# A decoder layer on one core: biased exponentials per head for the decay, DVE's linked operations as single steps, another split of the gelu sessions, new queue orders

## The chip, the cores and the metric

One core of one Trainium2 chip runs the whole program once. The metric is device time in microseconds (us) of that core; lower is better. Engines are named as in the profile: PE (TensorE), DVE (VectorE), ACT (ScalarE), POOL (GpSimd), and SP, which only issues DMAs.

## The reference

Input x is 16 samples of 128 tokens by 128 features, and there is a context of the same shape. One decoder layer with three layernorms is computed:

```
x = LN(x + attn(x))                 # 16 heads of 8; Q and K through a k=3 convolution and a projection
                                    # scores*tau + delta, with tau, delta = sigmoid(conv(gelu(dwconv(x))))
x = LN(x + xattn(x, ctx, ctx))      # mLSTM: 4 heads of 32
                                    #   D = exp(logD - max), C = qk*D/sqrt(32)
                                    #   norm = max(|sum C|, exp(-max logD)); per-head layernorm
x = LN(x + ffn(x))                  # blocks of 32 quantised to FP6 (scale = max|x|/7.5), one 128x128 linear
```

## The kernel before

Attention goes sample by sample (16), everything behind it group by group. `GR` lists 9 groups: seven of two samples (0 to 6), two of one (7 and 8). Projections and the convolution branches go by chunks of four samples (0 to 3). Every engine runs its own list of steps written out by hand (`PE_ORDER`, `DVE_ORDER`, `ACT_ORDER`, `POOL_ORDER`, `SP_ORDER`); a step is `name.index`. An engine takes its list strictly in order and each step waits on semaphores, so a step that is not ready holds up everything behind it on that engine.

**Front.** `tx.c` transposes chunk c of x on PE. `tapT`/`tapD` (two per chunk and branch, 16 in all) are the depthwise convolution: POOL writes the first tap, line 343, and DVE adds the two others, lines 995 and 996. `geT`/`geD` are the gelus on ACT (line 466), `tau`/`del` the projections on PE (lines 704, 713), `thT`/`thD` the tanh on ACT, `edx` exp(delta), `edT`/`edc` its transposition and copy. `K`, `Q` are projections of 6 matmuls each (line 627); `kf`, `qf` add the bias on DVE; `qs` multiplies q by tau; `km`, `qm` are masked copies for four heads on POOL (line 296). Gelu and exp lie in different activation tables: `gelu` and `exp` load one. The first table session is gelu for chunks 0 to 2, `exp.0` follows, then later `gelu.1`, the steps of chunk 3, and `exp.1`. POOL's tap for a chunk c from 2 on waits for `tau`/`del` of chunk c-2, whose buffer it takes. `zeros.0` (lines 333 to 335) clears the value buffers on POOL.

**Attention loop.** For sample n, `aa`/`v1`/`v2` hold the scores of n (`score_a`, line 633) and those of n-2 less their maximum (`score_b`, line 639, `less_max`, line 645) in four PSUM banks. `mX`/`mY` on DVE take the maxima (line 1054), `split` on POOL splits them into three bf16 parts, `nmT` transposes them, `eX`/`eY` on ACT are the exponentials (line 507), and `pv` (line 847, 64 small matmuls) multiplies by the values `vz` (DVE) and `ez` (POOL). `rec`, `att`, `y1` finish a group's attention (line 857 and 858).

**Behind it, for each group.** `y1s`, `sq1` (first layernorm), `yT`, `gb`, `l1`, `lf`, `gF`, `scan` (gates, cumulated); `spread` on SP writes the gate row to DRAM and reads it back on all partitions; `dm` on POOL masks it (line 391) and adds the column term g (line 393, 1024 columns); `dec` on ACT is one exponential of 1024 columns (line 560). Groups 7 and 8 (`BY_ROWS`) get their decay from PE (`ld`) and four exponentials with g as bias (line 567). `qk`, `cc` (decay times scores, DVE), `hst` (line 911), `hs`, `hq`; then `nrm`, `vs`, `rh`, `z2`, `bn`, `qa`, `zb` on DVE (with `rh`, `std` on ACT), `xd` (POOL), `dT`, `ffn` (PE), `z3` (DVE), `sq3` (ACT), `yo` (POOL, line 426) and `store` (SP). `cT`, `cm`, `gc` bring in the context. `warm.k` is k matmuls whose result nobody reads (line 917), all behind the last `att`.

`link(ins)` makes DVE wait for the instruction just issued; with it the steps `nrm` (3 links), `vs`, `z2`, `gb`, `bn`, `qa` (4) hold chains of small dependent operations within one step.

## Time and profile before

| | us |
|---|---|
| median of 3 runs | 234.24 |
| lowest and highest | 232.49, 236.56 |
| the profiled execution, its own time | 234.09 |
| its span, first to last instruction | 232.3 |
| PE busy | 206.4 (89%) |
| DVE busy | 169.7 (73%) |
| ACT busy | 128.6 (55%) |
| POOL busy | 115.2 (50%) |
| mean granted clock of PE | 0.977 |

A busy share is an average over the span; the front, the attention loop and the end have different limits. PE's digits in the profile's 40 slices run 2889397799799989998999999999997989999991, DVE's 2699999997824433559846798598697459998981.

### The profile page before, as it was taken

The page shows a single profiled execution, that of the slowest core. Times are in us where ns is not written, and L with a number is a line of the kernel's source. Part 1 is how long each engine was busy: PE and PEld are TensorE (multiplying, and loading weights), DVE is VectorE, ACT ScalarE, POOL GpSimd, SP SyncE. Part 2 cuts the span into 40 slices and gives each one's busy share as a digit, 9 for nine tenths or more (in the row PEclk, how much of TensorE's full clock was granted, in tenths as well). Part 3 has the DMA queues.
Part 4 walks back from the last instruction along what each step waited for, and adds up shares of the span by engine and source line. Part 5 has one row for each costly group of instructions (what it writes and reads, how often), then busy time and mean ns, then how long its engine had stood idle before and what let it go on. Part 6 is the DMA issues. An engine that isn't in the chain of part 4 may idle for free.

```text
span 232.3 us, 6553 instructions
## 1 busy us (share of the span) xinstructions
PE 206.4 (89%) x2377; PEld 137.6 (59%) x2377; DVE 169.7 (73%) x429; ACT 128.6 (55%) x365; POOL 115.2 (50%) x225
## 2 busy tenths in 40 slices
PE   2889397799799989998999999999997989999991
...
DVE  2699999997824433559846798598697459998981
...
GB/s 172 179 122 1 3 0 1 0 4 0 0 48 0 4 93 0 3 94 1 48 5 26 1 91 93 25 4 0 116 5 3 90 115 7 0 1 25 23 30 18
DMA packets 11311, 8.43 MB, mean 36 GB/s; under 512 B 2736, under 2 KB 10384, under 8 KB 11280
## 3 DMA queue, kind: packets, MB, share of 16 engines
...
HBM read 6.94 MB, written 1.08 MB: 35 GB/s over the span
## 4 chain that ended last, share of the span: by engine, by line
DVE 35%; PE 35%; issue 17%; POOL 7%; ACT 5%; POOLq 0%; DVEq 0%; ACTq 0%
PE bankPV L847 9%; PE score L633 6%; DVE u L995 5%; DVE u L996 4%; DVE nm L1054 4%; PE bankY L911 2%; PE score L639 2%; DVE z L1185 2%; PE bankP L704 2%; PE bankP L774 2%; PE score L645 2%; POOL qm L296 2%; DVE z L1164 1%; DVE mT L1157 1%; DVE hn L1140 1%
## 5 line engine op out<-in xcount | busy, mean ns | idle before, releaser
L1054 DVE TENSOR_REDUCE nm<-score 128x8 f32<-128x1024 f32 x32 | 38.8, 1219 | 9.3 <-PE score L633 9.3
L507 ACT ACTIVATE prob<-score 128x1024 f32<-128x1024 f32 x32 | 32.5, 1019 | 22.9 <-PE score L645 22.7
L633 PE MATMUL score<-km,qf 32*128 32x512 f32 x128 | 34.1, 642 | 1.2 <-DVE nm L1054 1.2
L639 PE MATMUL score<-qm,kf 32*128 32x512 f32 x128 | 34.3, 645 | 0.1
L466 ACT ACTIVATE u<-u,db 128x512 f32<-128x512 f32 x16 | 11.3, 719 | 19.0 <-DVE u L996 19.0
L645 PEld LDWEIGHTS score<-nmT,sel 32*128 32x128 bf16 x256 | 10.3, 95 | 16.7 <-issue 16.5
L296 POOL TENSOR_SCALAR km<-kf,mcol 128x512 f32<-128x512 f32 x16 | 13.9, 888 | 10.8 <-DVE kf L1031 5.6
L847 PE MATMUL bankPV<-prob,vz 128*32 128x128 f32 x512 | 18.7, 289 | 0.0
L917 PE MATMUL bankPV<-maskb,identb 128*128 128x512 bf16 x73 | 17.8, 380 | 0.0
L847 PE MATMUL bankPV<-prob,ez 128*32 128x128 f32 x512 | 17.3, 275 | 0.0
L627 PE MATMUL bankP<-xTp,wT 128*128 128x512 f32 x36 | 16.8, 602 | 0.4 <-ACT dth L476 0.4
L372 POOL CAST nmx<-nm 128x16 bf16<-128x16 f32 x16 | 3.2, 201 | 27.5 <-issue 19.7
L995 DVE SCALAR_TENSOR_TENSOR u<-xTp,dw,u 128x512 f32<-128x512 f32 x16 | 14.8, 927 | 2.2 <-POOL u L343 2.2
L911 PEld LDWEIGHTS bankY<-ctm,xt 128*128 128x128 f32 x128 | 15.1, 192 | 1.3 <-issue 0.8
L399 POOL TENSOR_SCALAR x<-y1s,rs 128x128 f32<-128x128 f32 x16 | 5.8, 375 | 20.1 <-DVE z L1164 14.0
L911 PE MATMUL bankY<-ctm,xt 128*128 128x33 f32 x128 | 15.8, 277 | 0.0
L343 POOL TENSOR_SCALAR u<-xTp,dw 128x512 f32<-128x512 f32 x16 | 13.9, 879 | 3.8 <-ACT xTp L454 2.7
L426 POOL TENSOR_SCALAR abT<-z,rs 128x128 f32<-128x128 f32 x16 | 5.9, 378 | 19.2 <-ACT rs L613 19.2
L847 PEld LDWEIGHTS bankPV<-prob,vz 128*32 128x32 f32 x512 | 14.1, 115 | 2.1 <-issue 0.8
L996 DVE SCALAR_TENSOR_TENSOR u<-xTp,dw,u 128x512 f32<-128x512 f32 x16 | 14.4, 902 | 0.6
L847 PEld LDWEIGHTS bankPV<-prob,ez 128*32 128x32 f32 x512 | 14.7, 112 | 0.1
L296 POOL TENSOR_SCALAR qm<-qf,mcol 128x512 f32<-128x512 f32 x16 | 12.6, 804 | 4.2 <-DVE qf L1041 4.2
...
## 6 DMA issues: line engine op xcount, KB each, us to landing
...
```

The costliest lines, as they stand in the source:

```text
L296: ins = nc.gpsimd.tensor_scalar(dst[:, CB * (c % 2):CB * (c % 2 + 1), j, :], src[:, CB * c:CB * (c + 1), :], mcol[:, j:j + 1], 1.0, ALU.mu ...
L507: nc.scalar.activation(prob[:, i % 2, k:k + 2, :].rearrange("p k s -> p (k s)"), sc[:, 512 * k:512 * (k + 2)], ACT.Exp, scale=SQ_SCALE).th ...
L627: ins = mm(place(name), wT[:, n, k, :], xTp[:, CB * c:CB * (c + 1), k:k + S], start=(k == 0), stop=(k == TAPS - 1))
L633: ins = mm(sc[:, 512 * k:512 * (k + 1)], qf[r, n, :], km[r, n % (2 * CB)].rearrange("p j s -> p (j s)"), start=True, stop=True)
L639: mm(sc[:, 512 * k:512 * (k + 1)], kf[r, n, :], qm[r, n % (2 * CB)].rearrange("p j s -> p (j s)"), start=True, stop=False)
L645: ins = mm(sc[:, 512 * k + S * j:512 * k + S * (j + 1)], sel[r, j, :], nmT[r, n % 3, :], start=False, stop=(j == J - 1))
L847: ins = mm(pvb[32 * k:32 * (k + 1), o:o + S], w[:, G * (i % 4) + k, 32 * j:32 * (j + 1)], prob[:, i % 2, k, S * j:S * (j + 1)], start=(j = ...
L911: ins = mm(yb[:, o:o + CW], cc[:, i % 2, S * k:S * (k + 1)], ctm[:, b0 + v, h, :], start=True, stop=True)
L917: mm(pvb[:], identb[:], maskb[:].unsqueeze(1).to_broadcast([P, NH, S]), start=True, stop=True)
L995: link(nc.vector.scalar_tensor_tensor(o, xTp[:, cs, 0:S], dw[:, n, j, 0:1], o, ALU.mult, ALU.add))
L996: nc.vector.scalar_tensor_tensor(o, xTp[:, cs, 2:S + 2], dw[:, n, j, 2:3], o, ALU.mult, ALU.add).then_inc(taps_done[n], 1)
L1054: nc.vector.tensor_reduce(nm[:, i % 3, J * k:J * (k + 2)], sc[:, 512 * k:512 * (k + 2)].rearrange("p (h s) -> p h s", s=S), AX_X, ALU.max, ...
```

## The change

1. `dm` keeps only its mask on POOL. `dec` for groups 0 to 6 becomes 8 exponentials of 128 columns, each with one column of g as bias, in place of one of 1024 columns. The groups 7 and 8 stay as they were.
2. The steps of DVE that held links are cut up: `gb` into `gb ga`; `nrm` into `na nb nrm`; `vs` into `v0 vs`; `z2` into `za z2`; `bn` into `ba bn be`; `qa` into `q0 q1 q2 q3 qa`. Each part has a semaphore, waits for the part before, and can stand anywhere in DVE's list. `hn8` and `st` get two buffers, so that waits for the group before become waits for the one before that. One of the four operations of `nrm` (maximum with the negated sum) goes; ACT takes the absolute value in a new step `ha` (128x8).
3. Gelu sessions: the first holds chunk 0 (`geT.0 geT.1 geD.0 geD.1`, and `geD.2`), then `exp.0` and four score exponentials of samples 0 and 1, then `gelu.1` with all other gelus and tanhs, then `exp.1`.
4. All five lists are new. `warm` falls from 73 matmuls to 46.

```
 PE_ORDER (before, first lines)
-    tx.0 ab.0 hw.0 mT.0 mT.1 wT.0 tx.1 del.0 tx.2 wT.1 tau.0 K.0 del.1 Q.0 Q.1 tx.3 del.2 aa.0 Q.2 gw.0 aa.1 tau.1 cg.0 nmT.0 ow.0 v1.2 nmT.1 K.1 edT.0
-    v2.2 edT.1 K.2 v1.3 V.0 edT.2 rc.0 v2.3 nmT.2 cT.0 pv.0 cm.0 v1.4 cm.1 pv.1 nmT.3 v2.4 V.1 y1.0 v1.5 nmT.4 tau.2 v2.5 gF.0 pv.2 v1.6 nmT.5 pv.3 tau.3
-    yT.0 del.3 MT.0 K.3 v2.6 edT.3 ...
+    tx.0 ab.0 mT.0 mT.1 hw.0 tx.1 tx.2 tx.3 wT.0 cT.0 wT.1 del.0 K.0 Q.0 tau.0 Q.1 gw.0 edT.0 aa.0 aa.1 K.1 nmT.0 cg.0 v1.2 nmT.1 ow.0 Q.2 v2.2 rc.0 K.2
+    v1.3 nmT.2 v2.3 K.3 del.1 nmT.3 tau.1 del.2 v1.4 tau.2 V.0 tau.3 pv.0 del.3 pv.1 V.1 v2.4 edT.1 cm.0 y1.0 edT.2 v1.5 edT.3 V.2 pv.2 yT.0 v2.5 nmT.4
...
 PE_ORDER (last lines)
-    v1.15 nmT.14 pv.12 v2.15 y1.5 cm.7 pv.13 nmT.15 bb.14 dT.3 cm.8 y1.6 gF.5 qk.4 ffn.3 MT.5 pv.14 yT.5 bb.15 gF.6 hst.4 qk.5 MT.6 y1.7 yT.6 pv.15 hst.5
-    yT.7 qk.6 y1.8 warm.6 gF.7 warm.8 dT.4 ld.7 ffn.4 warm.3 gF.8 qk.7 hst.6 warm.4 dT.5 ld.8 ffn.5 MT.7
-    warm.8 hst.7 warm.3 yT.8 warm.5 MT.8 qk.8 warm.5 dT.6 warm.4 ffn.6 warm.5 hst.8 warm.4 dT.7 warm.4 ffn.7 warm.14 dT.8 ffn.8
+    cm.7 v1.15 nmT.14 hst.3 dT.2 v2.15 ffn.2 cm.8 gF.5 qk.4 pv.13 MT.5 bb.14 nmT.15 hst.4 qk.5 y1.6 dT.3 pv.14 yT.6 bb.15 ffn.3 gF.6 y1.7 qk.6 pv.15 MT.6
+    hst.5 dT.4 y1.8 yT.7 warm.1 ffn.4 yT.8 warm.3 gF.7 warm.4 ld.7 qk.7 MT.7 hst.6 gF.8 qk.8 hst.7 dT.5 ld.8 MT.8 ffn.5 warm.5 hst.8 warm.8 dT.6 warm.3
+    ffn.6 warm.7 dT.7 warm.2 ffn.7 warm.11 dT.8 warm.2 ffn.8

 DVE_ORDER (first lines, and from the last att on)
-    cent.0 sel.0 ab.0 tapT.0 tapD.0 hw.0 mT.0 tapD.1 mT.1 tapT.1 wT.0 bias.0 tapD.2 tapT.2 tapD.3 tapT.3 wT.1 tapT.4 bias.1 kf.0 tapD.4 qf.0 tapD.5 qs.0
-    qf.1 tapT.5 wd.0 mY.0 mX.0 qf.2 gw.0 mX.1 mY.1 cg.0 qs.1 tapD.6 mX.2 tapD.7 ow.0 kf.1 tapT.6 mY.2 tapT.7 kf.2 mX.3 vz.0 rc.0 mY.3 gc.0 mX.4 ...
-    z2.4 gb.7 bn.4 att.8 qa.4 lf.7 nrm.5 zb.4 vs.5 scan.7 cc.6 gb.8 z2.5 lf.8 bn.5 z3.4 qa.5 scan.8 zb.5 cc.7 nrm.6 vs.6 z2.6 z3.5 bn.6 dd.7 qa.6 nrm.7
-    dd.8 vs.7 zb.6 cc.8 z2.7 bn.7 z3.6 qa.7 zb.7 nrm.8 vs.8 z3.7 z2.8 bn.8 qa.8 zb.8 z3.8
+    cent.0 sel.0 ab.0 tapT.0 mT.0 mT.1 tapD.0 hw.0 tapD.1 wT.0 tapD.2 wT.1 tapT.1 bias.0 wd.0 bias.1 kf.0 qf.0 tapT.2 tapD.3 qs.0 tapD.4 mX.0 mY.0 qf.1
+    gw.0 mY.1 mX.1 tapD.5 cg.0 kf.1 mX.2 ow.0 tapT.3 qf.2 tapT.4 mY.2 rc.0 tapT.5 mX.3 kf.2 mY.3 kf.3 qs.1 tapT.6 tapD.6 mX.4 tapT.7 tapD.7 vz.0 qs.2 ...
+    q3.4 qa.4 zb.4 gb.7 dd.6 att.8 ga.7 lf.7 v0.5 na.5 nb.5 nrm.5 vs.5 z3.4 gb.8 ga.8 za.5 z2.5 ba.5 scan.7 bn.5 cc.6 q0.5 lf.8 be.5 q1.5 dd.7 q2.5 q3.5
+    qa.5 cc.7 zb.5 scan.8 na.6 v0.6 nb.6 nrm.6 vs.6 v0.7 za.6 na.7 z2.6 nb.7 dd.8 ba.6 z3.5 cc.8 bn.6 nrm.7 q0.6 vs.7 be.6 q1.6 q2.6 q3.6 za.7 qa.6 z2.7
+    zb.6 na.8 ba.7 nb.8 v0.8 nrm.8 bn.7 vs.8 q0.7 be.7 q1.7 q2.7 z3.6 za.8 q3.7 qa.7 zb.7 z2.8 ba.8 z3.7 bn.8 q0.8 be.8 q1.8 q2.8 q3.8 qa.8 zb.8 z3.8

 ACT_ORDER (first lines)
-    xT.0 geT.0 geD.0 geD.1 xT.1 thD.0 geT.1 xT.2 geD.2 thT.0 geT.2 geD.3 geT.3 thD.1 geT.4 geD.4 geD.5 xT.3 thD.2 geT.5 thT.1 nmT.0 exp.0 edx.0 edx.1 ...
+    xT.0 geT.0 xT.1 xT.2 geD.0 xT.3 geD.1 cT.0 geD.2 thD.0 geT.1 thT.0 exp.0 edx.0 edc.0 nmT.0 eY.0 nmT.1 eX.0 eY.1 nmT.2 eX.1 gelu.1 geD.3 geT.2 geD.4
+    geT.3 thD.1 geT.4 nmT.3 geT.5 geD.5 thT.1 thD.2 geT.6 geD.6 thT.2 geT.7 geD.7 thT.3 thD.3 exp.1 eY.2 edx.1 rec.0 edx.2 edx.3 eX.2 edc.1 cm.0 y1s.0
...
 POOL_ORDER (first lines)
-    ident.0 consts.0 tapT.0 tapD.0 tapT.1 tapD.1 zeros.0 tapD.2 tapT.2 tapD.3 tapT.3 tapT.4 tapD.4 tapT.5 tapD.5 km.0 qm.0 split.0 tapD.6 split.1 tapD.7 ...
+    ident.0 consts.0 tapT.0 zeros.0 tapD.0 tapT.1 tapD.1 tapT.2 tapD.2 tapT.3 tapD.3 km.0 tapD.4 tapT.4 qm.0 tapT.5 split.0 tapD.5 ez.0 ez.1 split.1 km.1
+    split.2 xr.0 xr.1 xr.2 xr.3 km.2 split.3 tapT.6 tapD.6 tapT.7 qm.1 tapD.7 split.4 ez.2 x1.0 qm.2 split.5 ez.3 x1.1 split.6 km.3 dm.0 split.7 ez.4
```

```
 POOL, dm
-                    pool.wait_ge(g_done, i + 1)
                     t = dec[:, i % 2, 0:w * S].rearrange("p (h s) -> p h s", s=S)
-                    link(nc.gpsimd.affine_select(... fill=MASKED ...))
-                    nc.gpsimd.tensor_tensor(t, t, g[:, i % 2, 0:w].unsqueeze(2).to_broadcast([P, w, S]), ALU.add).then_inc(dm_done, 1)
+                    nc.gpsimd.affine_select(... fill=MASKED ...).then_inc(dm_done, 1)
 ACT, dec
-                    nc.scalar.activation(t, t, ACT.Exp).then_inc(dec_done, 1)
+                    for k in range(NH * GR[i][1]):
+                        t = dec[:, i % 2, S * k:S * (k + 1)]
+                        ins = nc.scalar.activation(t, pb[:, S * k:S * (k + 1)] if i in BY_ROWS else t, ACT.Exp, bias=g[:, i % 2, k:k + 1])
 ACT, new step ha
+                    nc.scalar.activation(ha[:, i % 2, 0:w], hs[:, i % 2, 0:w, DH], ACT.Abs).then_inc(ha_done, 1)
 DVE, nrm (before: four operations with three links)
-                    link(nc.vector.scalar_tensor_tensor(h1, hv, -1.0, h0, ALU.mult, ALU.max))
 DVE, qa (before: subtraction, link, quantise with three links inside); now
+                elif name == "q1":
+                    dve.wait_ge(q0_done, i + 1)
+                    nc.vector.tensor_reduce(qs8[:, i % 2, 0, 0:4 * nb], z[...], AX_X, ALU.max, apply_absolute_value=True).then_inc(q1_done, 1)
...
```

## Rows read from the trace of the kernel before

**Rows 1.** Busy time by stretch: window, its length, then each engine (instructions).
```profile
0.00:73.40 73.40, 58.49 (x442) 35.31 (x442) 57.51 (x107) 26.07 (x46) 51.38 (x93) 0.95 0.16 42
73.40:195.70 122.30, 116.59 (x1728) 82.62 (x1728) 83.09 (x218) 82.91 (x237) 53.45 (x113) 0.99 0.12 39
195.70:232.30 36.60, 31.30 (x210) 19.71 (x209) 29.10 (x106) 19.65 (x83) 10.35 (x21) 0.99 0.05 15
```

**Rows 2.** What PE waited for between 73.4 and 198.3 us: total, times, longest.
```profile
PE bankT L865 <- DVE dd L1122: 1.1, 1, 1.1
```

**Rows 3.** Timeline of PE: start, duration, work; first score of sample 5.
```profile
73.41 0.70 PE L633 MATMUL score<-km,qf 32*128 32x512 f32 x2
```

**Rows 4.** Timeline of PE: two context projections, then tau.3, del.3 and K.3.
```profile
65.88 0.73 PE L774 MATMUL bankP<-cen,cT 128*128 128x136 f32 x4
...
83.95 1.98 PE L704 MATMUL bankP<-u,xd 128*128 128x512 f32 x4
...
86.81 0.64 PE L713 MATMUL bankP<-u,d2w 128*32 128x128 f32 x16 [0.65 <-ACT th L472]
...
88.02 2.81 PE L627 MATMUL bankP<-xTp,wT 128*128 128x512 f32 x6 [0.42 <-ACT dth L476]
```

**Rows 5.** Groups of DVE instructions by line: count, busy us, mean ns, idle before.
```profile
L1054 DVE TENSOR_REDUCE nm<-score 128x8 f32<-128x1024 f32 x32 | 38.8, 1219 | 9.3 <-PE score L633 9.3
L995 DVE SCALAR_TENSOR_TENSOR u<-xTp,dw,u 128x512 f32<-128x512 f32 x16 | 14.8, 927 | 2.2 <-POOL u L343 2.2
L996 DVE SCALAR_TENSOR_TENSOR u<-xTp,dw,u 128x512 f32<-128x512 f32 x16 | 14.4, 902 | 0.6
```

**Rows 6.** Timeline of DVE: the first vz.
```profile
60.32 0.47 DVE L1068 TENSOR_TENSOR vz<-bankP,ed 128x128 f32<-128x128 f32 x2
```

**Rows 7.** POOL: the last memset of zeros.0 (timeline).
```profile
13.44 2.24 POOL L335 MEMSET ez<- 128x2560 f32 x1
```

**Rows 8.** POOL: groups by line, masks and the decay.
```profile
L296 POOL TENSOR_SCALAR km<-kf,mcol 128x512 f32<-128x512 f32 x16 | 13.9, 888 | 10.8 <-DVE kf L1031 5.6 <-PE score L633 5.1
L393 POOL TENSOR_TENSOR dec<-dec,g 128x1024 f32<-128x1024 f32 x7 | 13.6, 1940 | 0.6
```

**Rows 9.** Timeline of PE: del.1, then the six matmuls of Q.0.
```profile
27.05 1.08 PE L713 MATMUL bankP<-u,d2w 128*32 128x128 f32 x16 [3.45 <-issue]
28.17 3.89 PE L627 MATMUL score<-xTp,wT 128*128 128x512 f32 x6
```

**Rows 10.** Groups of ACT instructions by line: decay, exponentials, table loads.
```profile
L507 ACT ACTIVATE prob<-score 128x1024 f32<-128x1024 f32 x32 | 32.5, 1019 | 22.9 <-PE score L645 22.7
L560 ACT ACTIVATE dec<-dec 128x1024 f32<-128x1024 f32 x7 | 7.4, 1051 | 3.3 <-POOL dec L393 3.3
L459 ACT ACT_TABLE_LOAD x2 | 2.6, 1283 | 0.0
L567 ACT ACTIVATE dec<-bankP,g 128x128 f32<-128x128 f32 x8 | 2.3, 363 | 0.0
L480 ACT ACTIVATE dth<-dth,halfc 128x128 f32<-128x128 f32 x4 | 1.4, 391 | 0.0
```

**Rows 11.** Timeline of ACT: four per-head exponentials of group 7.
```profile
204.39 1.13 ACT L567 ACTIVATE dec<-bankP,g 128x128 f32<-128x128 f32 x4
```

**Rows 12.** Timeline of POOL: the decay's addition in group 4.
```profile
170.08 2.16 POOL L393 TENSOR_TENSOR dec<-dec,g 128x1024 f32<-128x1024 f32 x1
```

**Rows 13.** Timeline of DVE in the same stretch.
```profile
170.52 2.00 DVE L1164 TENSOR_TENSOR z<-mT,x 128x256 f32<-128x256 f32 x1
```

**Rows 14.** Timeline of DVE from the last att on.
```profile
195.70 0.29 DVE L1076 TENSOR_TENSOR att<-bankPV,rec 128x128 f32<-128x128 f32 x1
195.91 2.09 DVE L1185 TENSOR_SCALAR z<-z,mv 128x128 f32<-128x128 f32 x2
...
210.17 0.17 DVE L1141 SCALAR_TENSOR_TENSOR hn<-hn,se 128x8 f32<-128x8 f32 x1
...
226.55 0.29 DVE L949 TENSOR_TENSOR x<-z,qs 128x128 fp8e4<-128x128 f32 x1
```

More of the change, by code:

```diff
@@ L80 @@
-    thT.2 nmT.5 geD.7 thT.3 yT.0 thD.3 exp.1 eY.4 edx.3 em.0 rec.1 dec.0 eX.4 edc.3 y1s.1 sq1.1 eY.5 nmT.6 l1.1 eX.5 hs.0 hq.0 eY.6 em.1 rh.0 rec.2 nmT.7
-    eX.6 std.0 cT.1 dec.1 yT.1 eY.7 cT.2 dT.0 eX.7 nmT.8 cm.2 sq3.0 rec.3 nmT.9 cm.3 eY.8 cm.4 y1s.2 sq1.2 yT.2 y1s.3 l1.2 sq1.3 eX.8 l1.3 hs.1 hq.1 cm.5
-    rh.1 nmT.10 eY.9 std.1 eX.9 dec.2 em.2 rec.4 dT.1 cT.3 eY.10 em.3 cm.6 sq3.1 nmT.11 eX.10 dec.3 hs.2 yT.3 hq.2 eY.11 nmT.12 rh.2 eX.11 std.2 y1s.4
-    sq1.4 nmT.13 eY.12 l1.4 rec.5 dT.2 sq3.2 eX.12 em.4 hs.3 hq.3 yT.4 eY.13 nmT.14 rh.3 eX.13 std.3 dec.4 y1s.5 cm.7 sq1.5 nmT.15 rec.6 l1.5 eX.14 dT.3
```

197 lines of the change are left out of this document (118 added, 79 removed).

## The prediction

> **What bounds the kernel now.** Read the busy time by stretch first [rows 1]. I cut the span at the first score of sample 5 (`v1.5`, 73.41 us [rows 3]) and at the last `att` (195.70 [rows 14]). In the middle PE is busy for 116.6 of 122.3 us, DVE for 83.1, ACT for 82.9: PE bounds it, and of PE's 5.7 us of rest only a few are waits with a name, the longest 1.1 us for a `dd` that stood behind linked operations on DVE [rows 2]. In the front DVE is busy for 57.5 of 73.4 us, 29.2 of them the 16 pairs of taps [rows 5]; it is short of 100% only because the first eight and the last ten us are poor in DVE work. In the end, 36.6 us, DVE is busy for 29.1 with 106 small instructions, and ACT for 19.7. So three sums are needed: how early PE is filled, what is left of waits in the middle, how long DVE's list is behind the last `att`.
>
> **Front: new order and gelu sessions.** I take differences against the old list. Before the first `vz` (60.32 [rows 6]) old DVE had done 16 tap pairs, seven maxima, `kf`/`qf` 0 to 2, `qs` 0 and 1. New DVE up to `mY.3` has 12 pairs, eight maxima, no `qs.1`, and also `rc.0`. With the rows' means: minus 4 x 1.83 (927 and 902 ns), plus 1.2, minus 0.9, plus about 1.0 for `rc.0` (an estimate for its small operations), minus 2.2 that DVE waited for POOL's first taps [rows 5]. New is a wait for `tapD.0`: `zeros.0` is ahead of it on POOL, whose two memsets are 2.24 us each [rows 7], and of these 4.5 us DVE covers three with `tapT.0`, `mT.0`, `mT.1`; plus 1.6. `mY.3` then ends near 53.7.
>
> Here the new order has a chain. On POOL `km.2` (4 x 0.67 undisturbed, 0.89 on average [rows 8]) and `split.3` (about 1) follow; PE has `nmT.3` before `tau.1`; from the start of a `tau` to the end of its tanh it is 2.9 us (83.95 to 86.81 [rows 4]); `qs.1` waits for that, and so do POOL's `tapT.6`, which takes `tau.1`'s buffer, and the three other taps of chunk 3. That is 53.7 + 3.3 + 1 + 0.2 + 2.9 + 0.9 = 62.0 after `qs.1`, with DVE idle for some 6 us. Four tap pairs, `mX.4` and half a `vz`: + 7.3 + 1.2 + 0.3 = 70.8. ACT may leave the gelu session only after `thD.3`: `pv.0` about 2, `del.3` with its tanh 1.2 (86.81 to 88.02 [rows 4]), table 1.28, `eY.2` 1.02, three `edx` of 0.39 and one `rec` 0.8, `eX.2` 1.0 [rows 10]: `v1.5` starts at 79.3, minus 0.7 because `nmT.3` and `km.2` overlap DVE's `kf.3`: **78.6**, 5.2 later than now.
>
> But PE has more behind it by then: `tau.2` and `tau.3` (1.83 each, 83.95 to 85.78 where the next begins), `del.3` 0.6, `K.3` 2.8, and the waits of 0.65 and 0.42 beside them [rows 4], together 8.1, less `cm.1`, 0.7. That is 7.4 us that the middle no longer holds. **Front: 5.2 - 7.4 = -2.2 us.** Bounds: a pass over 512 columns cannot well take less than half of the 1.22 us of a maximum over 1024 [rows 5]; 15 pairs at 1.22 instead of 1.83 are 9.2 us less, so -11; on the other side, if each pair's two passes were held as long again as POOL's mask, 0.89 [rows 8], in 7 of the 15, 6.2 us later, so +4. I take the rows' mean, because POOL's masks and first taps still run beside these taps.
>
> **Middle: linked steps, POOL's addition, per-head exponentials.** POOL loses 7 x 1.94 = 13.6 us [rows 8]. It is not bound by these, but DVE was held up by them: `z2` of group 4, which begins 0.44 us after POOL's addition, took 2.00 us [rows 12, 13]. Nothing but the mask is left there. In a chain the links give one operation each 0.20 us, from 210.17 to the next [rows 14]; now other steps can stand between them. All this pays only where PE waits for DVE: the top wait was 1.1 [rows 2], all that PE was not busy is 5.7 [rows 1], of which 1.07 are counted above. So at most 4.6 are to be had.
>
> Against it stands ACT. One `dec` of 1024 columns is 1.05 us [rows 10]; four per-head ones of 128 columns are 1.13 together [rows 11], one every 0.26, so eight are 2.2: +1.1 for each of 7 groups, 7.7 in all. `ha`, nine of about 0.2: 1.8. ACT goes from 128.6 to about 138 busy. In the middle it is 83 of 122 and would be 90: not a bound in itself, but nothing else runs during a `dec`, and `eX.7`, `nmT.7` and `eX.11` are right behind one. The cover is that exponentials waited 22.9 us for PE in all [rows 10], not PE for them. If that cover were gone, five `dec` in the stretch would cost 5.5 us. The single instruction is 0.36 us from PSUM, and 0.39 for the nearest one from SBUF [rows 10]; both were issued overlapping. DVE's `ga`, `na` and so on have the same number of waits as the links had: no cost. **Middle: -1 us, between -4.6 and +5.5**: I take a quarter of the waits as gone, since the other engines have hardly less to do than before.
>
> By the Trainium skill, *ScalarE: Activation LUTs*, section "What ACT_TABLE_LOAD costs", an exponential with a per-partition bias has a fixed cost of 280 ns and 0.833 ns per column, and neighbours overlap by 93 ns. From that, eight are an estimated 2.44 us, and the seven decays would cost ACT 9.7 us instead of 7.7. The sum would stay, since ACT's time is covered; only the rival below would begin earlier.
>
> **End.** From the last `att` to the end of the last `qa` DVE now takes 195.70 to 226.84, 31.1 us, nearly always at work [rows 1, 14]. Taken out of this piece: `qa.4`, whose subtraction lasted 2.09 beside POOL's addition and which ends 3.4 us after it begins, `zb.4` 0.5, `gb.7` 0.2, and four times one linked operation, 0.8 [rows 14]: 4.9. Interleaving the rest (v0.7, na.7 between the steps of group 6, and so on) hides perhaps one in five of 40 links of 0.1: 0.8. Chain: `cc.8` and `hst.8` are now in front of `dT.6` and `ffn.6` on PE, so the last group is not late. From `qa.8` to the end stays 5.5 (226.84 to 232.30 [rows 1, 14]). **End: -5.5 us**, between 0 (what DVE no longer does is replaced by waits for `l1.8` and `dec.8`, two of which ACT serves later) and -9.
>
> **Sum.** -2.2 - 1 - 5.5 = -8.7: span 232.3 to 223.6. The profiled execution was 234.09, 1.8 over its span; it is 0.15 under the median. So 225.4; I say **225.5**.
>
> **Rivals.**
> - *The front pays as the lists intend.* DVE's taps are little disturbed and the wait for `tau.1` is short. For: taps and `km` no longer coincide everywhere. Against: the chain `km.2`, `split.3`, `nmT.3`, `tau.1`, `qs.1` is in the lists. Front -7, half way to its bound, end -7: 225.4 - 6.3 = 219.
> - *Nothing is gained.* PE gets its work earlier, but starves between 70 and 79 us, and the end stays bound by the chain of `ffn`, `sq3`, `yo`. Front 0, middle +2, end -3: 233. Part of it may be PE's clock: after 3.45 us without a matmul the six of `Q.0` took 3.89 us, those of `K.3` 2.81 [rows 9, 4], the lower of two levels (1.2 against 2.4 GHz) for part of it. In the end 27 of 73 `warm` are gone; if such a gap opens before `hst.7`, `hst.8` or `dT`, each costs about 1 us, four cost 4: 229.5. The Trainium skill says the same of idle stretches (*TensorE: Matmul & The Clock Gate*, "What's actually happening": idle, the array falls to 1.2 GHz); the granted clock now is 0.99 in the end [rows 1].
> - *ACT becomes the bound, slower than before.* Its place is each `dec` ahead of an `eX`, `eY` or `nmT` for which PE is ready. Price: eight at 0.39 not overlapping are 3.1, 2.1 more than one of 1.05 [rows 10]; seven and `ha` are 14.6 + 1.8 = 16.4 us: 225.4 + 16.4 = 242. It decides (over 239) once 13.5 of these are on the path. For: ACT is in order and PSUM banks of scores are freed by it alone. Against: one every 0.26 [rows 11], and ACT idle for 39 of 122 us [rows 1].
> - That the edit doesn't do what it says is not to be expected: it is instruction by instruction.
>
> **How the numbers follow.** Forecast, 221 to 229.6: 0.51. Front pays, 215 to 221: 0.16. Nothing gained, 229.6 to 238.9: 0.25. ACT the bound, above: 0.08. A change within 2% (229.6 to 238.9) could hardly be told from none. Faster 0.67, same 0.25, slower 0.08. The range 217.5 to 234 leaves out some 5 in 100 below, and 15 above: the last rival and the worse end of the one before. The forecast's own range is 221 to 229.6.
>
> **What would show it.** Right: `v1.5` between 76 and 80 us with `tau.3` and `K.3` before it, and a DVE gap of several us before `qs.1`; the last `att` near 193; from there to the end 31 us; no DVE operation of 2 us in the middle; eight exponentials in 2.2 us. Wrong: `v1.5` before 74 (front larger), named waits of PE for ACT of over 3 us in the middle (the third rival), or an end of over 34 us with DVE idle for more than 6 of them.

## The result and the profile after

The changed kernel takes 237.84 us (median of 4 runs, 236.12 to 240.90), the one before 234.07 beside it: a ratio of 1.019, with an interval of 1.013 to 1.025. The prediction was 225.5, range 217.5 to 234. It is slower, by an amount near the 2% that I took as the limit, and it lies outside the range. The profiled execution took 237.81 us, its span is 235.9 (before 232.3). In some executions of a kernel PE's mean granted clock is lower and the time some per cent longer: medians below are over all runs, ratios leave such runs out.

The span cut at the same two events as in [rows 1], the first score of block 5 (`v1.5`) and the last `att` (window, length, busy us of PE, its weight loads, DVE, ACT and POOL, each with its instructions, then granted clock, DMA share and GB/s):

```profile
0.00:88.83 88.83, 70.69 (x469) 41.88 (x469) 56.98 (x108) 32.44 (x54) 49.43 (x92) 0.94 0.13 35
88.83:199.39 110.56, 107.38 (x1717) 79.00 (x1716) 78.67 (x219) 84.12 (x278) 42.37 (x108) 0.98 0.12 38
199.39:235.90 36.51, 29.99 (x169) 19.55 (x168) 22.71 (x94) 20.73 (x93) 8.99 (x19) 0.84 0.11 33
```

`v1.5` comes 15.4 us later than before. 7.4 of these are work taken over from the middle, as in the prediction; 8.0 are a loss. The middle is 11.7 us shorter, 7.4 of it that work, so it gains 4.3. The end has 6.4 us less to do on DVE and is as long as before, with a granted clock of 0.84 in place of 0.99.

The front of the changed kernel in the timeline (start, duration, engine, line, work, and in brackets the idle time before and what ended it), from the table load on that opens the second gelu session:

```profile
59.42 1.28 ACT L458 ACT_TABLE_LOAD   x1
...
65.83 2.90 POOL L346 TENSOR_SCALAR u<-xTp,dw 128x512 f32<-128x512 f32 x3 [3.93 <-PE bankP L710]
66.38 0.69 DVE L1047 SCALAR_TENSOR_TENSOR qf<-th,qf 128x512 f32<-128x512 f32 x1 [4.54 <-ACT th L473]
...
71.56 0.72 ACT L467 ACTIVATE u<-u,db 128x512 f32<-128x512 f32 x1 [1.47 <-DVE u L1002]
...
73.00 0.68 PE L790 MATMUL bankP<-wvT,xTp 128*128 128x128 f32 x4 [2.38 <-ACT th L473]
...
75.72 0.48 DVE L1074 TENSOR_TENSOR vz<-bankP,ed 128x128 f32<-128x128 f32 x2
...
76.34 3.75 PE L710 MATMUL bankP<-u,xd 128*128 128x512 f32 x4 [2.66 <-DVE vz L1074]
80.02 1.40 PE L853 MATMUL bankPV<-prob,vz 128*32 128x128 f32 x32
...
83.20 1.28 ACT L460 ACT_TABLE_LOAD   x1
...
84.49 1.02 ACT L508 ACTIVATE prob<-score 128x1024 f32<-128x1024 f32 x1
...
85.66 0.70 PE L639 MATMUL score<-km,qf 32*128 32x512 f32 x2 [0.54 <-ACT prob L508]
```

From 59.42 to 83.20 ScalarE is in the gelu table, 23.8 us, busy for 11.7 of them; in the rest it waits for taps and for bank P. Its list has no exponential before `exp.1`, so the score banks stay full: `v2.4` (last row) waits for the exponential at 84.49. Behind `vz.0`, `tau.3` takes 3.75 us where it took 1.98 [rows 4]. PE had stood idle for 2.38 and 2.66 us before it (brackets above), and the granted clock from 76 to 80 us is 0.50, the lower level.

The end, in pieces of 4 us (same columns):

```profile
203.40:207.40 4.00, 3.41 (x22) 1.89 (x20) 3.40 (x14) 3.70 (x16) 0.66 (x2) 1.00 0.00 0
207.40:211.40 4.00, 3.29 (x31) 2.95 (x30) 3.62 (x13) 2.91 (x14) 1.33 (x3) 0.88 0.11 33
211.40:215.40 4.00, 4.00 (x23) 2.91 (x21) 1.34 (x8) 0.99 (x4) 0.82 (x2) 0.50 0.00 0
215.40:219.40 4.00, 4.00 (x16) 3.14 (x16) 2.25 (x10) 2.03 (x10) 0.66 (x2) 0.50 0.02 4
219.40:223.40 4.00, 4.00 (x21) 2.26 (x20) 3.87 (x16) 2.87 (x14) 1.77 (x4) 0.84 0.11 33
```

PE has gaps up to 208.4; from 210.5 to about 220.7 its granted clock is at the lower level, 1.2 GHz, and "busy 4.00 of 4" holds 16 to 23 matmuls. In the first full piece of that stretch DVE and ACT are busy for a third of the time or less; ACT waits there for PE (3.0 us in one wait), DVE for ACT and PE (1.8 and 1.1). Whether the whole end is longer for it is a question of its own, taken up below.

### The profile page after: what moved, and what is told of

The parts are those of the page before. It is cut to its first block, busy times and chain, and to the rows that moved or that the text cites. A ratio compares the mean times of both kernels' runs of the same rounds, so it can differ in the third digit from the quotient of the medians.

```text
span 235.9 us, 6548 instructions
## 1 busy us (share of the span) xinstructions
PE 208.1 (88%) x2350; PEld 140.4 (60%) x2350; DVE 158.4 (67%) x420; ACT 137.3 (58%) x423; POOL 100.8 (43%) x218
## 4 chain that ended last, share of the span: by engine, by line
PE 61%; issue 11%; DVE 11%; ACT 8%; DMA 4%; POOL 2%; SPq 1%; POOLq 0%; ACTq 0%; DVEq 0%
PE score L639 12%; PE bankPV L853 10%; PE bankY L917 6%; PE bankP L633 5%; PE score L633 3%; DVE u L1001 3%; DVE nm L1060 3%; PE bankP L710 2%; PE score L651 2%; ACT dec L567 2%; ACT prob L508 2%; DMA dec<-gates_out 2%; DVE u L1002 2%; PE score L896 2%; DMA pq<-in_L_attn_qproj_w_dram 1%
## 5 line engine op out<-in xcount | busy, mean ns | idle before, releaser
L639 PE MATMUL score<-km,qf 32*128 32x512 f32 x128 | 35.6, 677 | 5.4 <-DVE nm L1060 3.3
L645 PE MATMUL score<-qm,kf 32*128 32x512 f32 x128 | 34.5, 647 | 0.0
L853 PE MATMUL bankPV<-prob,vz 128*32 128x128 f32 x512 | 18.1, 285 | 0.7 <-ACT prob L508 0.7
L633 PE MATMUL bankP<-xTp,wT 128*128 128x512 f32 x36 | 17.5, 623 | 0.0
L346 POOL TENSOR_SCALAR u<-xTp,dw 128x512 f32<-128x512 f32 x16 | 14.8, 940 | 5.4 <-PE bankP L710 3.9
L567 ACT ACTIVATE dec<-dec,g 128x128 f32<-128x128 f32 x56 | 17.1, 391 | 0.0
L917 PEld LDWEIGHTS bankY<-ctm,xt 128*128 128x128 f32 x128 | 16.2, 203 | 1.2 <-issue 0.9
L639 PEld LDWEIGHTS score<-km,qf 32*128 32x128 f32 x128 | 9.6, 191 | 12.0 <-issue 8.5
L917 PE MATMUL bankY<-ctm,xt 128*128 128x33 f32 x128 | 16.8, 286 | 0.0
L853 PEld LDWEIGHTS bankPV<-prob,vz 128*32 128x32 f32 x512 | 13.8, 114 | 4.4 <-issue 2.1
L1001 DVE SCALAR_TENSOR_TENSOR u<-xTp,dw,u 128x512 f32<-128x512 f32 x16 | 14.2, 885 | 2.7 <-POOL u L346 2.7
L299 POOL TENSOR_SCALAR km<-kf,mcol 128x512 f32<-128x512 f32 x16 | 11.2, 716 | 9.7 <-DVE kf L1037 9.3
L1002 DVE SCALAR_TENSOR_TENSOR u<-xTp,dw,u 128x512 f32<-128x512 f32 x16 | 14.4, 902 | 0.6
```

The lines of the kernel that those rows point to most:

```text
L299: ins = nc.gpsimd.tensor_scalar(dst[:, CB * (c % 2):CB * (c % 2 + 1), j, :], src[:, CB * c:CB * (c + 1), :], mcol[:, j:j + 1], 1.0, ALU.mu ...
L346: nc.gpsimd.tensor_scalar(u[:, n, c % 2, j, :].rearrange("p (b s) -> p b s", b=CB), xTp[:, CB * c:CB * (c + 1), 1:S + 1], dw[:, n, j, 1:2] ...
L567: ins = nc.scalar.activation(t, pb[:, S * k:S * (k + 1)] if i in BY_ROWS else t, ACT.Exp, bias=g[:, i % 2, k:k + 1])
L633: ins = mm(place(name), wT[:, n, k, :], xTp[:, CB * c:CB * (c + 1), k:k + S], start=(k == 0), stop=(k == TAPS - 1))
L639: ins = mm(sc[:, 512 * k:512 * (k + 1)], qf[r, n, :], km[r, n % (2 * CB)].rearrange("p j s -> p (j s)"), start=True, stop=True)
L645: mm(sc[:, 512 * k:512 * (k + 1)], kf[r, n, :], qm[r, n % (2 * CB)].rearrange("p j s -> p (j s)"), start=True, stop=False)
```

## The experiments

The events of every profiled execution (us from the start of the span; the last column is span minus `v1.5`), in the order of the text below. "Time" is the median of the runs. The other columns are one execution each, and that one is not always typical: it took 4.7 us less than the median in h_front_before and 8.3 less in d_both, 5.0 more in a_end and 2.7 more in w_warm.

| kernel | time | v2.3 | v2.4 | v1.5 | last att | span | from v1.5 on |
|---|---|---|---|---|---|---|---|
| before | 234.1 | 60.25 | 70.54 | 73.41 | 195.70 | 232.3 | 158.9 |
| after | 237.8 | 56.62 | 85.66 | 88.83 | 199.39 | 235.9 | 147.1 |
| b_parts | 233.2 | 60.43 | 69.15 | 72.02 | 196.57 | 231.1 | 159.1 |
| b_decay | 235.6 | 60.80 | 71.02 | 73.89 | 198.29 | 233.3 | 159.4 |
| h_front_before | 233.4 | 60.67 | 69.40 | 72.26 | 190.46 | 226.8 | 154.5 |
| h_front_after | 244.0 | 54.02 | 84.02 | 88.06 | 205.74 | 240.3 | 152.2 |
| c_v0_early | 237.7 | 54.34 | 83.93 | 86.98 | 198.39 | 234.7 | 147.7 |
| c_chain | 236.3 | 58.07 | 85.04 | 88.21 | 198.22 | 236.0 | 147.8 |
| d_three | 251.7 | 53.63 | 79.78 | 82.84 | 210.04 | 249.8 | 167.0 |
| d_both | 249.8 | 53.94 | 69.99 | 77.57 | 203.40 | 239.6 | 162.0 |
| w_warm | 238.4 | 56.31 | 85.36 | 88.53 | 199.59 | 239.1 | 150.6 |
| h1_warm | 232.0 | 60.25 | 68.97 | 71.84 | 192.49 | 229.4 | 157.6 |
| a_end | 235.3 | 57.53 | 87.18 | 90.39 | 201.75 | 238.3 | 147.9 |
| mid_only | 232.0 | 60.74 | 72.53 | 75.39 | 193.51 | 229.9 | 154.5 |
| b_fewer_warm | 237.6 | 60.82 | 72.22 | 75.09 | 198.70 | 235.6 | 160.5 |
| a_end_46 | 242.9 | | | | | | |
| mid_46 | 235.8 | 61.02 | 70.42 | 73.29 | 191.85 | 234.1 | 160.8 |
| mid_shared | 243.5 | 61.76 | 72.41 | 75.28 | 204.05 | 242.0 | 166.7 |

Up to `v1.5` the kernels with the old front have the same lists, as far as PE is concerned, and yet `v1.5` lies between 71.8 and 75.4: from 60 to 70 us the granted clock is 1.00 in b_parts and 0.66 in mid_only and b_fewer_warm. Differences of 1 to 3 us between two profiled executions can come from that alone.

### Is it the code or the order?

**b_parts**: both code parts (per-head biased exponentials; linked operations as steps) with every order of the kernel before, the linked steps put one behind the other.

```
 DVE_ORDER: before's, with  gb.i -> gb.i ga.i   nrm.i -> na.i nb.i nrm.i   vs.i -> v0.i vs.i
            z2.i -> za.i z2.i   bn.i -> ba.i bn.i be.i   qa.i -> q0.i q1.i q2.i q3.i qa.i
 ACT_ORDER: before's, with  hq.i -> hq.i ha.i
```

> The kernel before with its own orders, but with both code parts of the change (per-head biased exponentials with POOL's addition gone; the linked operations of DVE as single steps, one right behind the other; ha right behind hq on ACT). Theory FRONT (the loss of the change is made before v1.5 by the new order and gelu sessions, about 8 us net; the parts cost nothing): 232 to 235 us. Rival PARTS (ACT's longer decay and ha are on the path, the orders are neutral): 237 to 240, like the changed kernel.

**b_decay**: the kernel before with the per-head exponentials alone.

```
-    link(nc.gpsimd.affine_select(out=t, ...))
-    nc.gpsimd.tensor_tensor(t, t, g[...].to_broadcast([P, w, S]), ALU.add).then_inc(dm_done, 1)
+    nc.gpsimd.affine_select(out=t, ...).then_inc(dm_done, 1)
-    nc.scalar.activation(t, t, ACT.Exp).then_inc(dec_done, 1)
+    for k in range(NH * GR[i][1]):
+        ins = nc.scalar.activation(t, ..., ACT.Exp, bias=g[:, i % 2, k:k + 1])
```

> The kernel before with its own orders, with the per-head biased exponentials alone (POOL's addition gone). ACT gets 17.1 - 7.4 = 9.7 us more to do. FRONT: within 1 us of before, the cover on ACT holds: 233 to 235. PARTS: 3 us or more slower, 237 or more, and PE's named waits for ACT prob appear as in the changed kernel (3.7 us).

**h_front_before**: the changed kernel, but its front in the order of before (PE up to `V.2`, DVE to `vz.2`, ACT to `sq1.1`, POOL to `dm.0`, SP to `spread.0`).

> Orders of before up to V.2 on PE and the matching places of the other engines (the second gelu session included), from there the new orders, with both code parts. FRONT: the 8 us of the front are gone and the gain of the middle stays (v1.5 to last att: 110.6 against 122.3 us, of which 7.4 are moved work, so 4.3): 234 - 4 = 230, 227 to 232. PARTS: 236 or more.

**h_front_after**: the reverse, the changed kernel's front (PE up to `edT.2`, DVE to `mY.4`, ACT to `sq1.0`, POOL to `x1.0`), then the order of before.

> The new orders up to edT.2 on PE and the matching places of the other engines (both gelu sessions included), from there the orders of before with the linked steps written out, with both code parts. FRONT: the loss of 8 us without the gain of the middle: 240 to 243. PARTS: as the changed kernel, 237 to 239. If the front costs nothing by itself: 234.

Measured: b_parts 233.17 us, ratio 1.001 (0.997 to 1.005); b_decay 235.58, 1.005 (1.000 to 1.010); h_front_before 233.44 (four runs, 228.8 to 236.8, its profiled one 228.76; no ratio); h_front_after 244.01, 1.047 (1.032 to 1.062). In the old order the code parts give nothing and cost nothing, as FRONT said (b_decay is 0.6 over its 233 to 235); h_front_after came out 1.0 above the 240 to 243 of FRONT. The new front alone costs 4.7%: its `v1.5` is 16.0 us behind that of b_parts, less the 7.4 of work it takes over 8.6, and the whole span is 9.2 longer. With the old front the rest of the new order takes 154.5 us from `v1.5` on, 4.6 less than b_parts. In the changed kernel it is 147.1 + 7.4 = 154.5 as well. So in these profiled executions the two pieces add up: front +8, everything behind it -4.4. The times bear out the front's loss, but less of the gain: the median of h_front_before, 233.4, is no better than that of b_parts, and the two kernels below that keep the old front and the new middle are 0.9 and 1.1% under b_parts by their ratios, 2.0 and 2.7 us.

That the exponentials are eight in place of one is seen in the busy time of ACT, not in the span (the group of instructions in the changed kernel: count, busy us, mean ns, idle time before it):

```profile
L567 ACT ACTIVATE dec<-dec,g 128x128 f32<-128x128 f32 x56 | 17.1, 391 | 0.0
```

17.1 / 7 is 2.44 us for eight. By the Trainium skill, *ScalarE: Activation LUTs*, "What ACT_TABLE_LOAD costs", I had put an estimated 2.44 beside my own 2.2; the trace agrees with it. PE's named waits for `prob` in the middle of b_decay are 1.3 us, not the 3.7 that PARTS wanted.

### What holds the scores in the new front

Up to `v2.3` the new front is ahead of the old one, by 3.6 us in the changed kernel and 6.2 in h_front_after. From `v2.3` to `v2.4` it takes 29.0 us, the old one 10.3. The question is what stands in these 29.

**c_v0_early**: in the changed kernel,

```
 PE  : ... K.3 [+V.0] del.1 nmT.3 tau.1 [+pv.0] del.2 v1.4 tau.2 [-V.0] tau.3 [-pv.0] del.3 pv.1 ...
 DVE : ... kf.3 [+vz.0] qs.1 tapT.6 tapD.6 mX.4 tapT.7 tapD.7 [-vz.0] qs.2 ...
```

> The changed kernel with three steps moved: V.0 to right behind K.3 and pv.0 to right behind tau.1 in TensorE's order, vz.0 to right behind kf.3 in VectorE's. CHAIN (the front is late because V.0 stands between tau.2 and tau.3, both of them in bank P, so that the last tau waits for a value evacuation, and pv.0 stands before del.3): v1.5 starts 4 to 7 us earlier than 88.8, at 82 to 85, and the time is 231 to 234. SESSION (the scores stand still because ScalarE can run no exponential before its second gelu session is over, and that session waits for the taps of VectorE, not for bank P): v1.5 moves by less than 2.5 us and the time is 235.5 to 238.

**c_chain**: the same, and

```
 ACT : ... geT.6 [+thT.2] geD.6 [-thT.2] geT.7 ...
 DVE : ... tapD.6 [-mX.4] tapT.7 tapD.7 [+mX.4] ...
```

> The same three steps moved, and two more: thT.2 ahead of geD.6 in ScalarE's order, mX.4 behind tapD.7 in VectorE's. CHAIN: these two add little, since V.0 was the stop: within 1.5 us of the kernel with three steps. SESSION: the taps of chunk 3 come 1.2 us earlier and th of chunk 2 1.5 us earlier, the session ends 3 to 6 us earlier than 83.2, v1.5 starts at 83 to 86, and the time is 2 to 3 us below that of the kernel with three steps.

Measured: c_v0_early 237.66 (ratio 1.018, 1.012 to 1.023); c_chain 236.31 (230.6 to 239.2). From `v2.3` to `v2.4` they take 29.6 and 27.0 us. Bank P as the one stop is refuted: with `V.0` and `pv.0` early this stretch is no shorter. The session as the one stop fits c_v0_early, where it ended at 80.4 and `tau.3` waited 3.86 us for a gelu. In c_chain only the stretch is 2 us shorter; `v1.5` at 88.21 missed the 83 to 86 of SESSION.

**d_three**: the session is cut in two and the second half, chunk 3, goes behind `eX.3`.

```
 ACT : ... thD.2 [+exp.1 eY.2 edx.1 ... eX.3 gelu.2] geT.6 geD.6 nmT.4 geT.7 thT.2 nmT.5 cT.1 geD.7 thT.3 thD.3 exp.2 ...
 PE  : tau.2 behind nmT.4; tau.3 del.3 behind pv.3; edT.3 behind v1.7
 DVE : qs.2 in front of qf.3      POOL: qm.2 behind split.6
```

> The changed kernel with its second gelu session cut in two: chunks 1 and 2 as before up to thD.2, then the exponentials of attention, and chunk 3 with thT.2 in a third short session behind eX.3; tau.2, tau.3, del.3, edT.3, qs.2, qm.2 and the chunk's row transposes move later with it. SESSION (the scores stand still for the 24 us in which ScalarE is in the gelu table and mostly waits for taps): the second session is under 10 us, v1.5 starts at 73 to 78 instead of 88.8, the stretch up to the last att gets back the 7 us of work moved behind v1.5 and 1.3 to 3 us for two more table loads, and the time is 228 to 233. BANK (something in TensorE's own order or in bank P holds the front): v1.5 starts after 83 and the time is 235 to 238.

Measured: 251.71 us (ratio 1.071, 1.059 to 1.083); `v1.5` at 82.84, beside the expected 73 to 78 and also beside "after 83". Neither theory was right. The timeline of this kernel shows the second gate:

```profile
64.63 1.28 ACT L462 ACT_TABLE_LOAD   x1
...
72.76 0.48 DVE L1076 TENSOR_TENSOR vz<-bankP,ed 128x128 f32<-128x128 f32 x2
...
73.45 1.93 PE L855 MATMUL bankPV<-prob,vz 128*32 128x128 f32 x32 [7.06 <-issue]
...
77.21 1.02 ACT L510 ACTIVATE prob<-score 128x1024 f32<-128x1024 f32 x1 [11.29 <-PE bankPV L855]
```

The session is over at 65.9, but the exponential waits another 11.29 us for `pv.0`: `prob` has two buffers, and `eY.2` overwrites that of block 0. `pv.0` waits for `vz.0`, which DVE has behind the eight tap passes (four pairs) of chunk 3.

**d_both**: d_three, and `V.0`, `vz.0`, `pv.0` moved as in c_v0_early.

> The kernel with the second gelu session cut in two, and with V.0, vz.0 and pv.0 moved as in the kernel with the early values. In the one alone the session ended at 64.6 and pv.0 started at 73.4, behind vz.0, which VectorE has behind the taps of chunk 3; the exponentials of block 2 then waited for pv.0, since prob has two buffers. In the other alone pv.0 was early and the session went on to 83. TWO GATES (the scores from block 4 on wait for the later of two things, the end of the gelu session and pv.0): with both moved v1.5 starts at 70 to 76, over 7 us earlier than in either alone, and then waits move behind it, as in the session kernel, so that the time stays over 236. ONE GATE ELSEWHERE: v1.5 starts at 80 or later.

Its timeline:

```profile
60.11 0.49 DVE L1076 TENSOR_TENSOR vz<-bankP,ed 128x128 f32<-128x128 f32 x2 [0.97 <-PE bankP L792]
...
63.85 1.08 PE L855 MATMUL bankPV<-prob,vz 128*32 128x128 f32 x32
...
66.69 1.28 ACT L462 ACT_TABLE_LOAD   x1
...
67.98 1.03 ACT L510 ACTIVATE prob<-score 128x1024 f32<-128x1024 f32 x1
...
74.64 0.97 PE L782 MATMUL bankP<-cen,cT 128*128 128x136 f32 x4 [1.99 <-DVE vz L1076]
```

`v2.4` starts at 69.99, 9.8 us before that of d_three and 13.9 before that of c_v0_early: two gates, of which the later one decides. Against the changed kernel's 85.66 the values moved alone give 1.7 us, the session cut alone 5.9, both together 15.7. `v1.5` at 77.57 just misses my 76: `vz.1` is still behind taps, and `cm.0` waits for it (last row). The whole is no better kernel, 249.78 us (241.5 to 250.8). It takes 162.0 us from `v1.5` on: from 84.56 to 100.83 ScalarE is in a third gelu session, 16.3 us, in which PE is busy for 11.7 and DVE for 2.6.

### The end: order, clock, or chain

**w_warm** and **h1_warm**: 19 more `warm` matmuls where the clock was at half, in the changed kernel, and in h_front_before.

```
-  ... warm.4 ld.7 qk.7 MT.7 hst.6 gF.8 qk.8 hst.7 dT.5 ld.8 MT.8 ffn.5 ...
+  ... warm.4 ld.7 warm.3 qk.7 MT.7 hst.6 warm.5 gF.8 warm.3 qk.8 hst.7 warm.5 dT.5 ld.8 warm.3 MT.8 ffn.5 ...
```

> The changed kernel with 19 more warm matmuls, put where TensorE's clock was at half in its last 25 us. CLOCK (the end won nothing because 27 warm matmuls are gone and TensorE ran at half clock for about 9 us of it): the granted clock of the last 36.5 us rises from 0.84 to above 0.95, the end shrinks by 3 to 4.5 us and the time is 233 to 235. WAITS (the end is set by the chain of VectorE and ScalarE, and TensorE had the slack for half speed): the end shrinks by less than 1 us and the time is 236.5 to 238.5.

> The front of the kernel before (to V.2), the rest of the changed kernel, and the 19 more warm matmuls. If both causes are right (the front as ordered loses 15 us up to v1.5, the end loses 3 to 4.5 to the clock): 223 to 226, where the front alone put back gave 228.8 in its profiled run and 233.4 at the median, and its runs agree better, since the lower ones of its clocks went with the longer times. If the clock does not matter in the end: 228 to 233.

Measured: w_warm 238.39, ratio 1.014 (1.008 to 1.021), not clearly different from 1.019; in its profiled execution the half clock stayed in part (0.50 from 211.6 to 215.6), and the end is 39.5 us. h1_warm 232.04, ratio 0.992 (0.989 to 0.996), 11 runs from 229.6 to 234.3: not the 223 to 226 I expected, but what was said for the case that the clock does not matter. Its profiled end fits that: beside h_front_before, which has the same orders and 19 fewer `warm`, the clock is back and the end is no shorter. First h_front_before, then h1_warm:

```profile
190.46:226.80 36.34, 29.99 (x168) 19.50 (x167) 22.93 (x94) 20.71 (x93) 9.04 (x19) 0.84 0.10 32
```

```profile
192.49:229.40 36.91, 31.40 (x187) 18.97 (x186) 22.12 (x94) 20.95 (x93) 9.27 (x19) 0.95 0.10 30
```

**b_fewer_warm**: b_parts with 46 of the 73 `warm`.

```
-  warm.6 8 3 4 8 3 5 5 4 5 4 4 14      (in the places of before, sum 73)
+  warm.1 7 0 0 0 0 0 5 8 3 7 4 11      (sum 46)
```

> Both parts of the code with all orders of the kernel before, and 46 warm matmuls in the end in place of 73, put where the changed kernel has them; b_parts with 73 gave 233.2, its last stretch 34.5 us at a granted clock of 0.98. CLOCK: with the 27 gone the clock falls to half somewhere in the last 30 us and the end is 2 to 4 us longer, 235 to 237. NO CLOCK: the warm matmuls are not needed here, the end is 34 to 35 us, 232.5 to 233.8.

**a_end**: the changed kernel up to `pv.15`, `att.8`, `rec.8`, `xd.4`, the rest in the order of before with 73 `warm`. **a_end_46**: the same with 46.

> The changed kernel up to pv.15 / att.8 / rec.8 / xd.4, and what is left in the order of the kernel before, with its 73 warm matmuls. ORDER (the end won nothing because the new order of the last groups is worse: the xd of group 6 comes 23.2 us behind the last att, 20.4 before): the stretch behind the last att is 31 to 34.5 us instead of 36.5, the time 232.5 to 235.5. CHAIN OF THE LAST GROUPS (each of the last three groups takes what it takes, the order does not matter, and neither does the clock): 36 to 37 us again, 236.5 to 239.

> The changed kernel with its end in the order of the kernel before, as the one that gave 235.3 (the changed kernel 237.8), but with 46 warm matmuls in place of 73. CLOCK (what that kernel won back came from the 27 warm matmuls): 1.5 to 4 us more than 235.3, at 237 to 239, with the granted clock of the stretch behind the last att at 0.80 to 0.88 in place of 0.98. ORDER (it came from the order of the last groups): 234.5 to 236.3, whatever the clock.

**mid_only**: front and end in the old order, the middle in the new one, both code parts, 73 `warm`. **mid_46**: the same with 46.

> The front of the kernel before (to V.2), the middle of the changed kernel, and the end again in the order of the kernel before with its 73 warm matmuls, with both parts of the code. ORDER: the end gets 2 to 5 us shorter than the 36.3 of the kernel with only the front put back, v1.5 stays at 72 and the middle at 118 to 120: 222 to 227. CHAIN OF THE LAST GROUPS: end 36 to 37, 228 to 232.

> Front and end in the old order, the middle in the new one, as the kernel that gave 232.0 (1.1% under the one before), with 46 warm matmuls in place of 73. CLOCK: 1.5 to 4.5 us more, 233.5 to 236.5, as between the two kernels with all orders of before (233.2 with 73, 237.6 with 46). ORDER: 230.5 to 233, since 27 matmuls of 0.2 us or so are gone and nothing waited for the clock.

Measured: b_parts 233.2 to b_fewer_warm 237.6 (ratio 1.020, 1.014 to 1.026); a_end 235.3 (1.007, 1.003 to 1.012) to a_end_46 242.9 (1.028, 1.022 to 1.035; its other runs 239.4 to 245.9, and one of 1029.8 that the last section tells of); mid_only 232.0 (0.989, 0.982 to 0.997) to mid_46 235.8 (1.009, 1.005 to 1.013). The medians are 4.4, 7.6 and 3.8 us apart. The 7.6 is too much, for the run of 1029.8 is one of the six behind that median; by the ratios the 27 matmuls taken out cost 1.9, 2.1 and 2.0%, 4.5 to 4.9 us in each of three kernels. All three have the end in the old order. Not all of it is seen in the end of the profiled executions: it grew from 34.5 to 36.9 us in b_fewer_warm (clock 0.98 to 0.84), and 3.1 us more lie ahead of `v1.5`, where the lists are the same; in mid_46 it grew by 5.9. First b_parts and b_fewer_warm:

```profile
196.57:231.10 34.53, 29.43 (x190) 18.03 (x182) 26.41 (x102) 20.24 (x90) 8.54 (x20) 0.98 0.05 16
```

```profile
198.70:235.60 36.90, 29.80 (x176) 19.32 (x175) 26.75 (x102) 20.65 (x91) 8.48 (x20) 0.84 0.05 15
```

Then the pieces of the end in mid_46 and, below, of mid_only:

```profile
191.85:234.10 42.25, 33.77 (x168) 22.79 (x167) 24.39 (x94) 21.18 (x93) 8.99 (x19) 0.75 0.08 28
203.00:207.00 4.00, 4.00 (x26) 3.82 (x19) 2.65 (x10) 0.78 (x4) 1.38 (x3) 0.50 0.11 33
207.00:211.00 4.00, 4.00 (x16) 2.90 (x14) 1.97 (x8) 2.59 (x10) 1.05 (x2) 0.50 0.00 0
```

```profile
193.51:229.90 36.39, 30.55 (x196) 19.52 (x194) 24.73 (x94) 21.19 (x93) 8.92 (x19) 0.97 0.10 31
...
209.00:213.00 4.00, 4.00 (x26) 2.60 (x26) 3.29 (x14) 3.30 (x16) 1.09 (x3) 1.00 0.01 1
```

The same list, but for the 27 `warm`, takes 42.3 us at 0.75 and 36.4 at 0.97. But also with the clock kept, the end behind the new middle is 36.4 (mid_only), not the 31 to 34 of ORDER, against 34.5 behind the old one (b_parts). In a_end it is as long:

```profile
201.75:238.30 36.55, 30.56 (x196) 19.50 (x195) 24.83 (x94) 21.18 (x93) 8.93 (x19) 0.98 0.10 31
```

So behind the new middle four profiled ends take 36.3 to 36.6 us, in the new order with 46 `warm` at 0.84 (h_front_before and the changed kernel) and in the old order with 73 at 0.97 and 0.98. By the times a_end is 1.1% under the changed kernel; its end changes order and `warm` together, and which of the two it is was not run apart. The chain of work that ended last in mid_only says what the end begins with (start, duration, what):

```profile
189.99 2.15 DMA gates_out<-nG
192.16 4.33 DMA dec<-gates_out
196.63 1.09 POOL dec L395
198.05 2.14 ACT dec L569 x7
```

The gates of group 6 go through memory, 6.5 us, then the mask and eight exponentials (the first at 197.75, seven on the chain). In b_parts the exponentials of that group start 0.5 us behind the last `att`, in mid_only 4.2 and in the changed kernel 4.9. The new order draws the last `att` forward, and this chain not as far: the middle looks shorter by what the end then waits. The two must be summed, and together they are 4.4 to 4.6 us less in the profiled executions of mid_only and h_front_before; by the ratio mid_only gains 1.1% on b_parts, 2.7 us, for its `v1.5` came 3.4 us later (75.4, with the clock at 0.66 from 60 to 70 us).

**mid_shared**: mid_only with the decay as before the change (one exponential, GpSimd's addition).

> Front and end in the old order, the middle in the new one, as in the kernel that gave 232.0, but with the decay as the kernel before has it: GpSimd masks and adds the gate, ScalarE does one exponential over the group. Per group ScalarE has one instruction of about 1.0 us in place of eight (2.44 us), GpSimd 2.16 us more. ORDER ALONE (the biased exponentials give nothing, as they gave nothing in the old order): 231 to 233.3. PORT (in the new order the add of GpSimd again stands beside VectorE's small operations and in front of the decay of group 6, which arrives 3 us behind the last att): 1 to 4 us more than 232.0, at 233.5 to 236.

Measured: 243.54, six runs, 234.8 (mean clock 0.977) to 247.7 (0.919); mid_only had 228.6 to 233.5. The middle is 128.8 us long instead of 118.1. ACT's waits from 72 us on (total, times, longest) now name GpSimd's decay, for which it waited 0.0 us in the changed kernel (group above):

```profile
ACT dec L565 <- POOL dec L398: 8.8, 4, 4.7
```

In mid_only ACT waited 1.9 us for POOL's mask in the same stretch. So in the new order the biased exponentials are worth something: its fastest run is 2.8 us over the median of mid_only, in the 1 to 4 of PORT. By the medians it is 11.6, more than either theory expected, but its runs lengthen as their clock falls, and how much of the 11.6 belongs to the clock is not separated. The size stays open.

## Why the prediction was wrong

**Front, the step that failed.** I put `v1.5` at 78.6 and the front at -2.2; measured 88.83 and +8.0. This 10.2 us is the largest part of the 12.3 between the span forecast, 223.6, and the measured 235.9; the middle came out 3.3 better than forecast, the end 5.4 worse. The 10.2 has three parts. (1) `mY.3` ended at 59.0, forecast 53.7. I had counted DVE's list, but from 8 to 32 us PE was busy for all 24.0 and DVE for 16.8 (before 19.3 and 22.8): the new list asks PE for more in this stretch (23.1 in d_both, whose start was quicker). Of the 5.3 us, 2.7 are the slower start of PE that this execution had (d_both, same order up to there, ended `mY.3` at 56.3), 2.6 the order. A quicker start is no cure: h_front_after ended `mY.3` at 56.4 and still reached `v1.5` at 88.06, for its `tau.1` took 3.40 us where the changed kernel's took 1.96. (2) From there to `vz.0` I had 17.1, measured 16.7: this chain, `km.2`, `split.3`, `nmT.3`, `tau.1`, taps, was right. (3) From `vz.0` to `v1.5` I had 7.8 and it took 13.1. My chain went from `vz.0` straight to `pv.0`, with no term for `tau.3`. But `V.0` stands between `tau.2` and `tau.3` and all three write bank P, so `tau.3`, its tanh and `del.3` come behind `vz.0`; from `vz.0` at 75.72 to `pv.0` at 80.02 it is 4.3 us, with `tau.3` at half clock for 3.75 of them. The rest took 8.8. With `V.0` early (c_v0_early) `tau.3` still waited for a gelu of chunk 3, and `v2.4` came only 1.7 us sooner: behind the missing term stands the chain through the taps. d_three and d_both show the structure that I did not see as a whole: blocks from 4 on wait for the later of the end of the gelu session and `pv.0`, and the new order puts both behind the taps of chunk 3. That the new front takes PE work over from the middle, 7.4 us, held: 147.1 and 154.5 differ by it.

**Middle, -1, measured -4.3, and end, -5.5, measured -0.1.** The sum -6.5 was 2.1 too good, each of the two far off; that they nearly cancel is luck. `att` was drawn forward, as said, but I took the end's length from DVE's list (31.1 us of work). DVE had 6.4 us less to do there (forecast 4.9 + 0.8), and then idled for 13.8 of 36.5 us. So the failed step of the end is the path: not DVE's list sets its length but a chain through group 6's gates (4.9 us before their exponentials begin) and then through PE and ACT. I had the missing `warm` matmuls as part of a rival, at 1 us each gap and 4 in all; a_end_46, mid_46 and b_fewer_warm measure 4.5 to 4.9 for their removal from the old end order. What they cost in the changed kernel's own end order stays open: w_warm did not restore the clock, and in h1_warm, where it was 0.95, the end was no shorter than at 0.84.

**Rivals.** "Nothing is gained" (233, chance 0.25) named both things that were seen, PE starving between 70 and 79 us and the lower clock in the end, and its band up to 238.9 holds the measured time; but it sized the front at 0 instead of +8. ACT as the bound is refuted: PE's named waits for ACT between 88.8 and 200 us are 1.4 + 0.7 us, for `prob` and not for `dec`, and b_parts, with eight exponentials in each of groups 0 to 6, takes the time of before. Of the signs named beforehand, the one against the forecast came true, an end of over 34 us with DVE idle for more than 6 of them. Of those for it, `v1.5` between 76 and 80 failed, and the DVE gap before `qs.1` was there (4.54 us), as was the absence of any DVE operation of 2 us in the middle, forecast from [rows 12, 13].

**A better version.** mid_only is faster than both kernels: 231.96, ratio 0.989 (0.982 to 0.997) against before; h1_warm does as well (0.992). The change's front order should be left out and the 73 `warm` kept. That is 1.1%, less than the 2% that I took as the limit. What loses is the new front; that the session split is the part of it that holds the scores is shown by d_three and d_both together, though neither is a faster kernel.
